# Edge loop of a four-layer GNN kernel: TensorE's transposes and second layer moved to the end of the loop body, blocks written out, one block bound loaded early

## The chip, the cores and the metric

One core of a Trainium2 chip runs one launch of the kernel. The metric is device time in microseconds (us) for the whole launch, the median of several runs. The engines are TensorE (PE; its weight loads are listed apart as PEld), VectorE (DVE), ScalarE (ACT), GpSimd (POOL) and SyncE (SP). Each engine has a sequencer that works through its instructions in order; the profile lists the sequencer's own work (register loads, branches) as PEldq, DVEq and ACTq. The engines tell each other of finished work by semaphores.

## What is computed

A residual network of four graph layers over 1024 nodes with 128 features and 16384 edges. The change lies in the stage that handles the edges, which serves all four layers:

```python
edge_index = jnp.stack([src, dst])
h = jnp.maximum(_layernorm(x), 0.0)
# layer 0, edge part: row = src, col = dst
m = jnp.concatenate([h[row], h[col]], axis=1)
m = relu(m @ Wm1 + bm1)
m = relu(m @ Wm2 + bm2)
m_sum = segment_sum(m, row, num_segments=1024)
# layer 1: attention over the edges, from edge counts per (src, dst)
# layer 2: mean over the first 10 edges of each source node
rank = arange(E) - starts[row_sorted];  keep = rank < 10
# layer 3: sum over the edges of edge_weight * x[src]
```

From the edges the kernel builds, beside `m_sum`, three dense tables over pairs of nodes: how many edges there are, how many of them are among a source's first ten, and the sum of their weights.

## The kernel before

**Staging.** The kernel first normalises `x` and sorts the edges by the block of 128 nodes in which their source lies (0 to 136 us of the span). A block's edges are padded to whole *pairs*: one pair is 2 x 128 edges. There are 8 blocks and, with this input, 68 pairs. Then the edge loop runs (150 to 573 us), and after it the node part of layer 0 and layers 1 to 3.

**The edge loop.** On TensorE, VectorE and ScalarE alike it is an outer loop over the 8 blocks with an inner loop over the block's pairs `g`, from `g0` to `end`. Both bounds are read from the tile `tabs` into registers by `value_load` at the start of each block. On TensorE and VectorE the outer loop is a loop of the machine (`eng.Fori(0, NB)`), and the place in `tabs` is itself worked out from the register `b`; on ScalarE the 8 blocks are written out by Python. GpSimd's part is written out over all pairs and has no blocks.

**TensorE, one pair** (lines 1195 to 1233): the transposes of pair `g+1`'s messages (L1140, into bank 6), the second layer of pair `g` (L1147 and L1148, into bank 7), `ranks` with `notbefb` (L1153, "ranks A", waits for `ranks_read`), a register load of the pair's `span` (L1204), `sources` for pair `g+2` (L1162, into bank 5), the inner loop that adds counts and weights into banks 0 to 3 (L1216 and L1219), the message sums (L1225, into bank 4), and `ranks` with `beforeb` for the next pair (L1153, "ranks B", signals `ranks_done`).

**VectorE, one pair**: reads the ranks (L880, waits for `ranks_restarted` and `ranks_done`, signals `ranks_read`), makes `OHc` (L885, L888), adds the bias to bank 7 (L891), makes the message of pair `g+2` (`message`, L864), and makes the next pair's one-hot tiles `OHs` (L900) and `OHd` (L905). **ScalarE, one pair**: `OHe` (L537), `OHs32` (L539), the two ReLUs (L549, L552).

**Between two blocks** the accumulated banks are emptied. ScalarE copies banks 2 and 3 (L557) and bank 4 (L558). VectorE copies banks 0 and 1 to `cntf` (L908, signals `counts_out`), makes `CT` (L911) and `SK` (L913), and waits for its own `kept_out`. TensorE waits for `counts_out` and `msum_out`, clears banks 0 to 4 with five matmuls by zeros (L1238), loads its two bounds (L1190, L1191) and restarts the ranks (L1153, signals `ranks_restarted`).

**The order** is that of the program text on each engine. No scheduler moves anything.

In the rows, tiles that share memory have the name of the larger one: `SK` is shown as `n1T`, the zeros as `hn`, bank tiles as `PS`, the gathered messages as `BT`.

Of the kernel before, what the change touches and what calls it, by code (L numbers as in the profile page):

```python
# [22 lines left out]
NB = N // P  # L23
# [3 lines left out]
NPAIR = E // PAIR + NB  # L27
# [30 lines left out]
def gnn_kernel(nc, I, out):  # L58
    ctx = ExitStack()
    with ctx:  # L60
        sems = {}

        def S(name):

            if name not in sems:
                sems[name] = ctx.enter_context(nc.semaphore(name))
            return sems[name]
# [180 lines left out]
        none = sb("none", [P, NB])  # L248
        lone = sb("lone", [P, P], bf16)
        zT = TT[0]  # L250

        block = ctx.enter_context(nc.Block())

# [204 lines left out]
        def _(eng):  # L458
# [74 lines left out]
            def scaled_onehots(g):  # L533
# [4 lines left out]
                eng.wait_ge(S("pair_done"), g + 1)  # L538
                a.activation(OHs32[:], OHs[:], ACT.Copy).then_inc(S("scaled_ready"), 1)  # L539

            for b in range(NB):
                g0 = eng.value_load(tabs[0:1, b:b + 1], min_val=0, max_val=NPAIR - 2)
                end = eng.value_load(tabs[0:1, b + NB:b + NB + 1], min_val=1, max_val=NPAIR - 1)
                with eng.Fori(g0, end) as g:
                    eng.wait_ge(S("src_onehots"), g + 1)
                    eng.wait_ge(S("counts_added"), g + 1)
                    scaled_onehots(g)
                    eng.wait_ge(S("m2_biased"), g + 1)
                    a.activation(m2s[:], m2s[:], ACT.Relu).then_inc(S("m2_ready"), 1)  # L549

                    eng.wait_ge(S("t_done"), g + 2)
                    a.activation(m1T[:].rearrange("p k e -> p (k e)"), bank(6), ACT.Relu).then_inc(S("m1_ready"), 1)  # L552

                eng.wait_ge(S("ranks_done"), end + 1)
                if b >= 2:
                    eng.wait_ge(S(f"spilled{b % 2}"), 16 * (b // 2))
                a.activation(TT[b % 2], bank(2, 2), ACT.Copy).then_inc(S("weights_out"), 1)  # L557
                a.activation(msum[:, :, b * P:(b + 1) * P], bank(4)[:, 0:F2].rearrange("p (f n) -> p f n", f=2),  # L558
                             ACT.Copy)\
                    .then_inc(S("msum_out"), 1)  # L560
            for b in range(NB):
                eng.wait_ge(S("SKT_done"), b + 1)
                a.activation(SKT[:, :, b * P:(b + 1) * P],
                             bank(6 + b % 2).bitcast(bf16).rearrange("p (j n) -> p j n", j=NB), ACT.Copy,
                             scale=1.0 / FRAC).then_inc(S("SKT_ready"), 1)
# [109 lines left out]
        def _(eng):  # L675
# [193 lines left out]
            eng.wait_ge(S("t_done"), 1)  # L869
            eng.wait_ge(S("pparts_done"), 2)  # L870
            v.tensor_tensor(MS[:], made, G[:, 1, :, :], ALU.add).then_inc(S("msg_ready"), 1)
            with eng.Fori(0, NB) as b:
                g0 = eng.value_load(tabs[0:1, bass.ds(b, 1)], min_val=0, max_val=NPAIR - 2)
                end = eng.value_load(tabs[0:1, bass.ds(b + NB, 1)], min_val=1, max_val=NPAIR - 1)
                with eng.Fori(g0, end) as g:

                    eng.wait_ge(S("ranks_restarted"), b + 1)
# [26 lines left out]
                    for k in range(2):  # L904
                        v.tensor_scalar(OHd[:, k, 0:N], iotaN[:], dstf[:, bass.ds(2 * g + 2 + k, 1)], None, ALU.is_equal)  # L905

                eng.wait_ge(S("ranks_done"), end + 1)
                v.tensor_copy(cntf[:], bank(0, 2)).then_inc(S("counts_out"), 1)  # L908
                eng.wait_ge(S("counts_out"), b + 1)
                ct = CT[:, bass.ds(b, 1), :].rearrange("p o n -> p (o n)")  # L910
                v.tensor_copy(ct, cntf[:]).then_inc(S("ct_out"), 1)  # L911
                eng.wait_ge(S("ct_out"), b + 1)
                v.tensor_tensor(SK[:, bass.ds(b, 1), :].rearrange("p o n -> p (o n)"), cntf[:], ct, ALU.subtract)\  # L913
                    .then_inc(S("kept_out"), 1)
                eng.wait_ge(S("kept_out"), b + 1)


            v.sem_inc(S("msg_ready"), NB)
            link(v.reciprocal(rden[:], Ur[:, :, D]))
# [126 lines left out]
        def _(eng):  # L1046
# [139 lines left out]
            transposes()  # L1186
            eng.wait_ge(S("turned_onehots"), 2)
            sources(1, second)
            with eng.Fori(0, NB) as b:
                g0 = eng.value_load(tabs[0:1, bass.ds(b, 1)], min_val=0, max_val=NPAIR - 2)  # L1190
                end = eng.value_load(tabs[0:1, bass.ds(b + NB, 1)], min_val=1, max_val=NPAIR - 1)  # L1191
                eng.wait_ge(S("src_onehots"), g0 + 1)
                ranks(((0, beforeb, 0), (1, onesb, 0), (1, beforeb, 1))).then_inc(S("ranks_restarted"), 1)
                with eng.Fori(g0, end) as g:
                    eng.wait_ge(S("m1_ready"), g + 1)
                    eng.wait_ge(S("msg_ready"), g + 2)
                    transposes()
                    second_layer(0)
                    second_layer(1).then_inc(S("m2_done"), 1)

                    eng.wait_ge(S("ranks_read"), g + 1)
                    ranks(((0, notbefb, 0), (0, onesb, 1), (1, notbefb, 1))).then_inc(S("ranks_added"), 1)
                    eng.wait_ge(S("spans"), 1)
# [28 lines left out]
                    eng.wait_ge(S("src_onehots"), g + 2)  # L1232
                    ranks(((0, beforeb, 0), (1, onesb, 0), (1, beforeb, 1))).then_inc(S("ranks_done"), 1)

                eng.wait_ge(S("counts_out"), b + 1)
                eng.wait_ge(S("msum_out"), b + 1)
                for k in range(5):
                    t.matmul(bank(k), zeros[:, 0:P], zeros[:, 0:BANK], start=True, stop=True)  # L1238

            eng.wait_ge(S("kept_out"), NB)  # L1240
            for b in range(NB):
# [244 lines left out]
```

## Time and profile before

| | |
|---|---|
| median of 3 runs | 1013.98 us (1013.17 to 1014.08) |
| profiled execution, its own time | 1013.37 us |
| its span, first to last instruction | 1011.5 us |
| PE busy | 834.6 us (83%) |
| DVE busy | 695.8 us (69%) |
| ACT busy | 476.0 us (47%) |
| mean granted TensorE clock | 0.947 of full |

The span is 1.9 us shorter than the execution's own time; what lies around it is not touched here. Busy times are means over stages with different limits, so the edge loop has to be read by itself, in order of time, on two or three engines at once. The words in brackets behind a row say how long the engine had been idle and what ended that; "issue" means that it waited for nothing that the profile knows as work, which in this kernel is mostly the engine's own sequencer with a register load or a branch.

### The profile page before, as it was taken

The numbers are of one execution on the slowest core, as the hardware profiler recorded it, in microseconds if no ns is written. First come the engines' busy times: TensorE is split into PE (matmuls) and PEld (weight loads), VectorE is DVE, ScalarE is ACT, GpSimd is POOL, SyncE is SP. The second block draws the span as 40 slices with busy tenths as digits, with TensorE's granted clock in tenths as the row PEclk, the third lists the DMA queues.
The fourth block names the chain that finished last, engine by engine and source line by source line (L and its number), as shares of the span: only waits on it lengthen the run. The fifth ranks groups of instructions, "written<-read, shape, count | busy, mean of one in ns | idle before, by whom it ended". The sixth has DMA issues, their size and how long they took to land.

```text
span 1011.5 us, 18259 instructions
## 1 busy us (share of the span) xinstructions
PE 834.6 (83%) x5207; PEld 523.3 (52%) x5236; DVE 695.8 (69%) x1803; ACT 476.0 (47%) x979; POOL 316.5 (31%) x424
## 2 busy tenths in 40 slices
PE   3999969989898989898989796877877766776658
PEld 2556738868787878686868644411142112311124
DVE  6399986666666666666666763699568875998451
ACT  5232105555555555564546655354544544445421
POOL 5030047545444545454535400122233120122000
PEclk9999969999999999999999999799879997999879
DMA  3120032111111111111112200000000000000300
GB/s 79 39 68 1 1 124 64 47 57 52 52 51 53 52 57 47 62 42 62 47 57 46 58 1 1 1 0 1 0 1 1 1 0 1 0 1 0 129 38 21
DMA packets 19139, 35.76 MB, mean 35 GB/s; under 512 B 5281, under 2 KB 11553, under 8 KB 18977
## 3 DMA queue, kind: packets, MB, share of 16 engines
q0 software_dynamic: 7104, 19.41, 6.7%
q1 hardware_dynamic: 12000, 15.95, 4.7%
q8 instruction: 15, 0.25, 0.1%
q14 instruction: 20, 0.16, 0.1%
HBM read 29.56 MB, written 5.79 MB: 35 GB/s over the span
## 4 chain that ended last, share of the span: by engine, by line
PE 63%; DVE 21%; ACT 6%; issue 5%; POOL 4%; DMA 0%; DVEq 0%; POOLq 0%; ACTq 0%
DVE OHd L964 9%; PE PS L1225 7%; PE PS L1147 6%; PE PS L1148 6%; PE PS L1219 5%; PE PS L1162 5%; DVE PS L975 5%; PE PS L1097 4%; PE PS L1337 4%; PE PS L1140 3%; PE PS L1262 3%; PE PS L1216 3%; PE PS L1153 2%; PE PS L1298 2%; PE PS L1328 2%
## 5 line engine op out<-in xcount | busy, mean ns | idle before, releaser
L390 POOL DMA_INDIRECT BT<-Qtab,gidx x148 | 150.5, 1017 | 96.3 <-DVE gidx L789 61.2
L537 ACT ACTIVATE OHe<-OHs,sew 128x128 bf16<-128x128 bf16 x408 | 126.7, 389 | 56.1 <-PE PS L1225 52.6
L404 POOL TENSOR_SCALAR KV<-BT,pid 128x256 bf16<-128x256 uint8 x74 | 70.3, 950 | 180.0 <-DVE MS L864 175.2
L964 DVE CUSTOM_DVE_ANT_0 OHd<-PS,n1T 128x1024 bf16<-128x1024 f32 x96 | 113.4, 1219 | 18.6 <-PE PS L1298 18.6
L549 ACT ACTIVATE m2s<-m2s 128x512 f32<-128x512 f32 x68 | 42.8, 630 | 119.1 <-DVE m2s L891 119.1
L1328 PE MATMUL PS<-rowA,sel 128*128 128x512 bf16 x177 | 57.9, 407 | 48.6 <-DVE PS L975 38.6
L443 POOL TENSOR_TENSOR zl<-AL,Sx 128x8 f32<-128x8 f32 x12 | 11.3, 946 | 258.7 <-DVE Sx L964 258.7
L891 DVE TENSOR_TENSOR m2s<-PS,bm 128x512 f32<-128x512 f32 x68 | 47.0, 691 | 59.0 <-PE PS L1148 58.8
L905 DVE TENSOR_SCALAR OHd<-iotaN,dstf 128x1024 bf16<-128x1024 f16 x136 | 64.6, 515 | 33.2 <-PE PS L1225 33.2
L1147 PE MATMUL PS<-Wm,m1T 128*128 128x256 f32 x272 | 83.8, 391 | 0.0
L1148 PE MATMUL PS<-Wm,m1T 128*128 128x256 f32 x272 | 82.6, 386 | 0.0
L1225 PE MATMUL PS<-OHs,m2s 128*128 128x128 f32 x544 | 78.1, 286 | 0.0
L630 ACT ACTIVATE Wn<-PS,s 128x1024 f32<-128x1024 f32 x48 | 53.1, 1113 | 49.3 <-PE PS L1328 49.1
L1097 PE MATMUL PS<-KV,m2s 128*128 128x288 f32 x256 | 72.8, 430 | 2.8 <-DVE KV L781 2.6
L1219 PE MATMUL PS<-OHd,OHe 128*128 x852 | 75.1, 220 | 0.0
L1328 PEld LDWEIGHTS PS<-rowA,sel 128*128 128x128 bf16 x192 | 11.8, 99 | 115.9 <-DVE PS L975 81.6
L864 DVE TENSOR_TENSOR MS<-PS,BT 128x512 f32<-128x512 f32 x68 | 47.0, 692 | 32.1 <-PE PS L1162 32.1
L1225 PEld LDWEIGHTS PS<-OHs,m2s 128*128 128x128 f32 x544 | 65.8, 191 | 5.1
L975 DVE SCALAR_TENSOR_TENSOR PS<-msum,s,BT 128x1024 f32<-128x1024 f32 x48 | 61.3, 1290 | 8.5 <-ACT cntf L630 5.2
L1162 PE MATMUL PS<-SKT,KV 128*128 (+1 forms) x420 | 59.4, 278 | 8.8 <-POOL KV L404 5.2
L1216 PE MATMUL PS<-OHd,OHc 128*128 x284 | 62.7, 221 | 4.4 <-issue 0.7
L781 DVE SCALAR_TENSOR_TENSOR KV<-iota,hi,carried 128x288 f32<-128x288 f32 x128 | 65.5, 512 | 0.0
(342 smaller groups left out, 1668.7 us busy)
## 6 DMA issues: line engine op xcount, KB each, us to landing
BT<-Wtab SPq DMA_DIRECT2D x1, 4096.0 KB, 12.9
BT<-Qtab,gidx POOLq DMA_INDIRECT x148, 2.8
BT<-Stab SPq DMA_DIRECT2D x1, 2048.0 KB, 10.2
Wtab<-H SPq DMA_DIRECT2D x4, 512.0 KB, 2.8
Wtab<-cs SPq DMA_DIRECT2D x4, 512.0 KB, 2.9
Qtab<-BT SPq DMA_DIRECT2D x1, 1024.0 KB, 4.5
Wn<-in_L_gnn_Wn SPq DMA_DIRECT2D x1, 1024.0 KB, 5.5
x<-in_x SPq DMA_DIRECT2D x1, 512.0 KB, 4.3
```

What stands on the lines that cost most here:

```text
L390: g.indirect_dma_start(out=G[:, p % SLOTS, k, :], out_offset=None, in_=Qtab, in_offset=bass.IndirectOffsetOnAxis(ap=gidx[:, p, k:k + 1], a ...
L537: a.activation(OHe[:, k, j, :], OHs[:, k, :], ACT.Copy, scale=sew[:, j, bass.ds(2 * g + k, 1)])
L964: v.tensor_tensor_reduce(junk[n % 2], bank(4, 2), mask[:, i, :], 1.0, 2 * FAR, ALU.subtract, ALU.max, Sx[:, i, hd:hd + 1]).then_inc(S("gat ...
L975: v.scalar_tensor_tensor(tile(hd, j), drow[hd], s8[:, j, hd:hd + 1], LNC[:, j, :], ALU.max, ALU.add).then_inc(S("gat_tt"), 1)
L1097: t.matmul(bank(5)[:, 0:2 * NCH], OHlo[:, i % RING, :], KV[:, i % RING, :, :].rearrange("p k c -> p (k c)"), start=(i == 0), stop=(i == T ...
L1147: t.matmul(to, m1T[:, k, :], Wm2[:, 0, :], start=True, stop=False)
L1148: return t.matmul(to, m1T[:, 2 + k, :], Wm2[:, 1, :], start=False, stop=True)
L1162: last = t.matmul(bank(5)[:, k * F2:(k + 1) * F2], OHsT[:, slot, k * P:(k + 1) * P], Pp[:, blk, j, :], start=(j == 0), stop=(j == 2))
L1216: t.matmul(PS[:, bass.ds(at, P)], OHc[:, k, :], dst, start=False, stop=False, skip_group_check=True)
L1219: t.matmul(PS[:, bass.ds(at + 2 * BANK, P)], OHe[:, k, j, :], dst, start=False, stop=False, skip_group_check=True)
L1225: last = t.matmul(bank(4)[:, f * P:(f + 1) * P], m2s[:, k, f * P:(f + 1) * P], OHs32[:, k, :], start=False, stop=False, skip_group_check=True)
L1328: last = t.matmul(tile(hd, j)[:, half * BANK:(half + 1) * BANK], sel[:, half, :], rowA[:, hd % 2, :], start=False, stop=False, skip_group_ ...
```

## The change

- On TensorE, the transposes and the second layer become a function `layers(g)`. It is called once ahead of the blocks with `g = 0`, and in the loop body for `g + 1` at the end, behind ranks B. The order of the work is the same around the loop; the place at which the loop closes, and at which a block ends, is now behind the second layer. Over the whole loop `layers` runs once more than before.
- On TensorE and VectorE the 8 blocks are written out by Python in place of the loop of the machine, as they were on ScalarE.
- All three engines load one bound per block in place of two: `g0` is the `end` of the block before. The load of the next block's `end` stands directly behind the inner loop, ahead of the waits that empty the banks. The place in `tabs` is a constant.

```diff
+        def last_pair(eng, b):
+            return eng.value_load(tabs[0:1, NB + b:NB + b + 1], min_val=1, max_val=NPAIR - 1)
...
 # VectorE (ScalarE likewise)
-            with eng.Fori(0, NB) as b:
-                g0 = eng.value_load(tabs[0:1, bass.ds(b, 1)], min_val=0, max_val=NPAIR - 2)
-                end = eng.value_load(tabs[0:1, bass.ds(b + NB, 1)], min_val=1, max_val=NPAIR - 1)
+            g0, end = 0, last_pair(eng, 0)
+            for b in range(NB):
                 with eng.Fori(g0, end) as g:
...
+                after = last_pair(eng, b + 1) if b + 1 < NB else None
                 eng.wait_ge(S("ranks_done"), end + 1)
                 v.tensor_copy(cntf[:], bank(0, 2)).then_inc(S("counts_out"), 1)
...
                 eng.wait_ge(S("kept_out"), b + 1)
+                g0, end = end, after
 # TensorE
+            def layers(g):
+                eng.wait_ge(S("m1_ready"), g + 1)
+                eng.wait_ge(S("msg_ready"), g + 2)
+                transposes()
+                second_layer(0)
+                second_layer(1).then_inc(S("m2_done"), 1)
+
+            layers(0)
+            g0, end = 0, last_pair(eng, 0)
+            for b in range(NB):
                 eng.wait_ge(S("src_onehots"), g0 + 1)
                 ranks(((0, beforeb, 0), (1, onesb, 0), (1, beforeb, 1))).then_inc(S("ranks_restarted"), 1)
                 with eng.Fori(g0, end) as g:
-                    eng.wait_ge(S("m1_ready"), g + 1)
-                    eng.wait_ge(S("msg_ready"), g + 2)
-                    transposes()
-                    second_layer(0)
-                    second_layer(1).then_inc(S("m2_done"), 1)
-
                     eng.wait_ge(S("ranks_read"), g + 1)
...
                     ranks(((0, beforeb, 0), (1, onesb, 0), (1, beforeb, 1))).then_inc(S("ranks_done"), 1)
+                    layers(g + 1)
+
+                after = last_pair(eng, b + 1) if b + 1 < NB else None
                 eng.wait_ge(S("counts_out"), b + 1)
                 eng.wait_ge(S("msum_out"), b + 1)
                 for k in range(5):
                     t.matmul(bank(k), zeros[:, 0:P], zeros[:, 0:BANK], start=True, stop=True)
+                g0, end = end, after
```

TensorE at the end of a block, before: from the message sums past the end of the inner loop (L1194) to the clearing matmuls (L1238) and the end of the outer loop (L1189).

```order
L1225 MATMUL PS<-OHs,m2s 128x128 x4
L1153 MATMUL PS<-OHs,beforeb 128x128
L1153 MATMUL PS<-OHs,onesb 128x128
L1153 MATMUL PS<-OHs,beforeb 128x128
L1194 REGISTER_ALU
L1194 COMPARE_AND_BRANCH
L1235 REGISTER_ALU
L1238 MATMUL PS<-hn 128x512 x5
L1189 REGISTER_ALU
L1189 COMPARE_AND_BRANCH
```

The same place after the change (the inner loop is now L1206, `value_load` L254, the clearing L1247):

```order
L1156 MATMUL PS<-OHs,beforeb 128x128
L1143 MATMUL PS<-ident,MS 128x128 x4
L1150 MATMUL PS<-Wm,m1T 128x256
L1151 MATMUL PS<-Wm,m1T 128x256
L1150 MATMUL PS<-Wm,m1T 128x256
L1151 MATMUL PS<-Wm,m1T 128x256
L1206 REGISTER_ALU
L1206 COMPARE_AND_BRANCH
L254 TENSOR_LOAD tabs
L254 ISA x2
L1247 MATMUL PS<-hn 128x512 x5
L1204 REGISTER_ALU
```

Transposes and second layer now stand between ranks B and the clearing; before, they stood behind the restart of the ranks in the next block.

VectorE at the end of a block, before:

```order
L875 COMPARE_AND_BRANCH
L907 REGISTER_ALU
L908 COPY cntf<-PS 128x1024
L909 REGISTER_ALU
L911 ISA
L911 COPY CT<-cntf 128x1024
L913 REGISTER_ALU
L913 TENSOR_TENSOR n1T<-cntf,CT 128x1024
L872 REGISTER_ALU
L872 COMPARE_AND_BRANCH
```

VectorE after the change (the inner loop is L879, the copies L913, L915 and L917):

```order
L879 COMPARE_AND_BRANCH
L254 TENSOR_LOAD tabs
L254 ISA x2
L912 REGISTER_ALU
L913 COPY cntf<-PS 128x1024
L915 CAST CT<-cntf 128x1024
L917 TENSOR_TENSOR n1T<-cntf,CT 128x1024
L879 UNCONDITIONAL_BRANCH
L882 REGISTER_ALU
```

The one load left stands ahead of the first copy; behind the last there is no load, and the jump back of the outer loop is gone.

## Rows read from the trace of the kernel before

**Rows 1.** Timeline of PE: start us, us, what, count, [idle before <- what ended it].

```profile
199.88 0.22 PE L1153 MATMUL PS<-OHs,beforeb 128*128 128x128 bf16 x1
...
202.22 0.22 PE L1153 MATMUL PS<-OHs,notbefb 128*128 128x128 bf16 x1
...
205.37 0.22 PE L1153 MATMUL PS<-OHs,beforeb 128*128 128x128 bf16 x1
...
207.39 1.02 PE L1238 MATMUL PS<-hn 128*128 128x512 bf16 x4 [1.70 <-DVE cntf L908]
...
209.50 0.23 PE L1153 MATMUL PS<-OHs,beforeb 128*128 128x128 bf16 x1 [1.08 <-issue]
...
212.02 0.22 PE L1153 MATMUL PS<-OHs,notbefb 128*128 128x128 bf16 x1
...
213.23 0.88 PE L1162 MATMUL PS<-SKT,KV 128*128 x6 [0.88 <-issue]
...
216.24 0.22 PE L1153 MATMUL PS<-OHs,beforeb 128*128 128x128 bf16 x1
```

**Rows 2.** Timeline of DVE: the same end of a block, and a pair in the third.

```profile
200.35 0.27 DVE L880 CUSTOM_DVE_ANT_0 prod<-OHs,PS 128x128 f32<-128x128 bf16 x1
...
205.84 1.21 DVE L908 COPY cntf<-PS 128x1024 f32<-128x1024 f32 x1
...
207.20 0.69 DVE L911 CAST CT<-cntf 128x1024 f32 x1
...
208.02 1.23 DVE L913 TENSOR_TENSOR n1T<-cntf,CT 128x1024 f32 x1
...
211.31 0.29 DVE L880 CUSTOM_DVE_ANT_0 prod<-OHs,PS 128x128 f32<-128x128 bf16 x1 [2.06 <-issue]
...
216.75 0.27 DVE L880 CUSTOM_DVE_ANT_0 prod<-OHs,PS 128x128 f32<-128x128 bf16 x1
...
260.48 0.29 DVE L880 CUSTOM_DVE_ANT_0 prod<-OHs,PS 128x128 f32<-128x128 bf16 x1 [2.04 <-issue]
...
266.26 0.27 DVE L880 CUSTOM_DVE_ANT_0 prod<-OHs,PS 128x128 f32<-128x128 bf16 x1
```

**Rows 3.** Waits, 150 to 572 us: engine line <- cause: us in total, times, longest.

```profile
DVE prod L880 <- issue: 15.8, 8, 2.1
```

**Rows 4.** DVE's sequencer, L872 to L875: count, ns min/median/max, first start, last start.

```profile
L875 DVEq COMPARE_BRANCH  x1: 50/50/50, 205.2 to 205.2; - x1
...
L872 DVEq FUSED_REGOPS  x1: 70/70/70, 209.6 to 209.6; - x1
...
L873 DVEq TENSOR_LOAD <-tabs x8: 301/306/566, 152.3 to 519.4; - x8
...
L874 DVEq FUSED_REGOPS  x2: 57/124/190, 210.3 to 210.7; - x2
...
L875 DVEq MOVE  x1: 43/43/43, 211.0 to 211.0; - x1
```

**Rows 5.** Timeline of PE and DVE at the first pair of the first block.

```profile
152.87 1.12 PE L1140 MATMUL PS<-ident,MS 128*128 128x128 f32 x4 [1.29 <-DVE MS L871]
...
154.32 0.29 DVE L880 CUSTOM_DVE_ANT_0 prod<-OHs,PS 128x128 f32<-128x128 bf16 x1 [1.51 <-issue]
...
156.94 0.22 PE L1153 MATMUL PS<-OHs,notbefb 128*128 128x128 bf16 x1
...
160.03 0.28 DVE L880 CUSTOM_DVE_ANT_0 prod<-OHs,PS 128x128 f32<-128x128 bf16 x1
```

**Rows 6.** Timeline of PE behind the last block.

```profile
573.70 1.07 PE L1245 MATMUL PS<-identb,n1T 128*128 128x128 bf16 x16 [0.90 <-DVE n1T L913]
```

**Rows 7.** Stretch: us, busy us (x) of PE, PEld, DVE, ACT, POOL, PEclk, DMA, GB/s.

```profile
258.50:262.50 4.00, 3.71 (x13) 3.10 (x14) 1.09 (x7) 0.00 (x0) 0.00 (x0) 0.57 0.11 32
```

**Rows 8.** DMA, 160 to 570 us: queue: packets, MB, share; issue: count, us to landing.

```profile
q14 instruction: 4, 0.03, 0.0%
...
BT<-Qtab,gidx POOLq DMA_INDIRECT x137, 2.8
```

More of the change, by code:

```diff
@@ L539, in scaled_onehots @@
                 a.activation(OHs32[:], OHs[:], ACT.Copy).then_inc(S("scaled_ready"), 1)
+            g0, end = 0, last_pair(eng, 0)
             for b in range(NB):
-                g0 = eng.value_load(tabs[0:1, b:b + 1], min_val=0, max_val=NPAIR - 2)
-                end = eng.value_load(tabs[0:1, b + NB:b + NB + 1], min_val=1, max_val=NPAIR - 1)
                 with eng.Fori(g0, end) as g:
@@ L909, in _ @@
                 eng.wait_ge(S("counts_out"), b + 1)
-                ct = CT[:, bass.ds(b, 1), :].rearrange("p o n -> p (o n)")
-                v.tensor_copy(ct, cntf[:]).then_inc(S("ct_out"), 1)
+                v.tensor_copy(CT[:, b, :], cntf[:]).then_inc(S("ct_out"), 1)
                 eng.wait_ge(S("ct_out"), b + 1)
-                v.tensor_tensor(SK[:, bass.ds(b, 1), :].rearrange("p o n -> p (o n)"), cntf[:], ct, ALU.subtract)\
-                    .then_inc(S("kept_out"), 1)
+                v.tensor_tensor(SK[:, b, :], cntf[:], CT[:, b, :], ALU.subtract).then_inc(S("kept_out"), 1)
                 eng.wait_ge(S("kept_out"), b + 1)
+                g0, end = end, after
             v.sem_inc(S("msg_ready"), NB)
@@ L1188, in _ @@
             sources(1, second)
-            with eng.Fori(0, NB) as b:
-                g0 = eng.value_load(tabs[0:1, bass.ds(b, 1)], min_val=0, max_val=NPAIR - 2)
-                end = eng.value_load(tabs[0:1, bass.ds(b + NB, 1)], min_val=1, max_val=NPAIR - 1)
+            def layers(g):
[5 more added lines that the diff above has]
+            layers(0)
+            g0, end = 0, last_pair(eng, 0)
+            for b in range(NB):
                 eng.wait_ge(S("src_onehots"), g0 + 1)
@@ L1233, in _ @@
                     ranks(((0, beforeb, 0), (1, onesb, 0), (1, beforeb, 1))).then_inc(S("ranks_done"), 1)
+                    layers(g + 1)
+                after = last_pair(eng, b + 1) if b + 1 < NB else None
                 eng.wait_ge(S("counts_out"), b + 1)
@@ L1238, in _ @@
                     t.matmul(bank(k), zeros[:, 0:P], zeros[:, 0:BANK], start=True, stop=True)
+                g0, end = end, after
             eng.wait_ge(S("kept_out"), NB)
```

## Prediction

> **What bounds the kernel now.** I read the edge loop in order of time, first TensorE, then VectorE over the same stretch, then VectorE's sequencer. Inside a block TensorE's matmuls follow each other with next to no gap: one pair takes 205.37 - 199.88 = 5.49 us from ranks B to ranks B [rows 1]. Across the end of a block the same distance is 216.24 - 205.37 = 10.87 us [rows 1], so emptying and restarting costs 5.4 us, seven times between 8 blocks. In that stretch TensorE waits three times: 1.70 us for `cntf`, 1.08 us and 0.88 us for its own sequencer [rows 1]. But TensorE is not what ends last there. VectorE copies from 205.84 to 209.25 without a gap that matters, and only at 211.31 reads the ranks of the next pair, after 2.06 us of "issue" [rows 2]. TensorE had restarted the ranks at 209.50 [rows 1], nearly 2 us earlier, and the transposes and second layer that it ran meanwhile held nobody up: ranks A at 212.02 came 0.71 us behind L880, and the span load and `sources` at 213.23 behind that [rows 1, 2]. So the chain over a block's end is: ranks B, VectorE's three copies, VectorE's two register loads, L880, ranks A. All eight such waits together are 15.8 us; the first is 1.51 us, so the seven between blocks are 2.04 us each [rows 3, 5].
>
> What the 2.06 us hold is seen in the sequencer. The copies end at 209.25; the jump of the outer loop is over at 209.6, the first load's part runs from there to 210.3, the second's to 211.0, and the set-up of the inner loop takes the last 0.3 us [rows 2, 4]. One load with its address and check is thus 0.7 us, of which 0.31 is the load itself.
>
> **Loads and jump on VectorE.** Behind the copies go both loads (2 x 0.7) and the outer jump. What stays is the wait for `kept_out` (about 0.1 of the 0.35 up to 209.6, my split) and the set-up of 0.3, so 0.4 in place of 2.06: 1.66 us less per block. One load comes back ahead of the first copy. The inner loop is left at 205.25 [rows 4]; 0.6 us (0.7 less the address, now a constant) make it 205.9, and a register operation and the start of the copy about 206.05, where the copy now starts at 205.84 [rows 2]. That is 0.2 us late. One of the eight loads took 0.57 in place of 0.31: the first, issued as VectorE had just begun a long operation [rows 4], and here L905 is running; with that the copy is 0.45 late. I take 0.3. The least is nothing, if the load lies wholly under L905. The most is a load that waits until L905 is through, which is at about 205.84: then the copy is 0.9 late. Net per block 1.66 - 0.3 = 1.35 us, from 0.75 to 1.66. Queued behind this load on VectorE are only the copies, and for them wait TensorE's clearing and, in the end, L880.
>
> **TensorE at the same place.** The question is whether it becomes the last. From ranks B to ranks A of a pair, with transposes and second layer between, it is 202.22 - 199.88 = 2.34 us [rows 1]. So the moved work ends at 205.37 + 2.34 = 207.71, later than the 207.39 at which clearing starts now, but it stands under VectorE's copies. The five clearing matmuls take 1.07 (four are 1.02 with the last one's tail), the ranks restart at 208.8, and L880 could start 0.47 later (199.88 to 200.35 [rows 1, 2]) at 209.25. VectorE gets there only at 211.31 - 1.35 = 209.95. TensorE has 0.7 us in hand. Its own load falls while the second layer runs. From L880 on everything depends on L880 as today: ranks A after 0.71, `sources` after 1.92, next L880 after 216.75 - 211.31 = 5.44 [rows 1, 2], because the layers, gone from this pair's front, were under that wait anyway. So their move gives nothing beyond letting VectorE's gain through: had they stayed, the second layer would end at 209.50 + 2.5 = 212.0 and hold ranks A there. **Both parts are needed, and together they give 7 x 1.35 = 9.5 us.** ScalarE's load lies in its wait for ranks B and costs nothing; GpSimd's order isn't touched.
>
> **Inside a block** the sequence is the same, with the jump now between second layer and ranks A. TensorE's sequencer runs ahead of the matmuls there, waiting for `ranks_read`. I count nothing.
>
> **The start.** Here the move costs. Before, the ranks of pair 0 were restarted ahead of the layers, while TensorE waited for the message (transposes at 152.87), and VectorE read them at 154.32 [rows 5]. Now the restart stands behind `layers(0)`, where ranks A stood, at 156.94; L880 comes 0.47 later at 157.4, and the next one 5.44 later at 162.85, against 160.03 [rows 5]: 2.8 us lost. From below: L880 is 3.1 us later, and ranks A of this pair comes at 158.1 in place of 156.94, 1.2 us; as the remainder had slack of its own I take 2.0 as the least, and 3.4 as the most.
>
> **The end.** `layers` runs once more behind the last ranks B, 2.3 us. By the times of block 0 the layers and the clearing are through 2.34 + 1.07 = 3.4 us behind ranks B. TensorE's next work waits for VectorE's last copy, `n1T` [rows 6], which is through 209.25 - 205.37 = 3.9 us behind ranks B [rows 1, 2] and has no load ahead of it in the last block. Cost nothing, with 0.5 us in hand.
>
> **The clock.** After two of the seven ends the granted clock fell for some 3.4 us; one stretch of 4 us shows 0.57 of full [rows 7], so 1.2 GHz for most of it, and the pair in it took 266.26 - 260.48 = 5.78 against 5.44, 0.34 us [rows 2]. The change leaves TensorE less idle at these places: the two falls may go (0.7 us less), or, as everything shifts, two others come (0.7 more). I count nothing.
>
> **Sum.** The profiled execution took 1013.37 us, 0.6 below the median of the runs: 1013.37 - 9.5 + 2.8 = 1006.7. Against the median it would be 0.6 more; I stay with the profiled one. Bounds: 1013.37 - 11.6 + 2.0 - 0.7 = 1003.1, and 1013.37 - 5.3 + 3.4 + 0.7 = 1012.2.
>
> **Rival 1: early loads are not early.** VectorE's load waits for L905, and TensorE's for its second layer (clearing at 208.4, L880 at 210.0 or later), so a good part of the 2.06 us is only moved: 0.75 per block, 1013.37 - 5.3 + 2.8 = 1010.9. For it: the one load of 0.57. Against: seven of eight, and that one too, took nothing like a whole operation. 0.12.
>
> **Rival 2, slower: code is fetched again.** Eight bodies stand where one stood on TensorE and VectorE. If a body lies across the border of two pieces of code and the jump back has to fetch the first again, every pair of that block pays. The nearest price of a small transfer is 2.8 us to landing [rows 8], the least nothing. One such block on one engine has 8.5 pairs: 24 us, 1030; from three paid fetches on, the 6.7 us are gone. Against: in 68 passes through three loops, ScalarE's written out eight times already, four packets of instructions came, 8 KB each [rows 8], so no loop fetched per pass. For: ScalarE's bodies are short. 0.06. The Trainium skill, Runtime: NRT & Kernel Launch, Instruction fetch mechanics, says that code comes in 16 KiB blocks, that two are held, and that a taken branch out of them stalls for a fetch. By that rule a body on TensorE that leaves the two would give this rival's time; the trace, with packets of 8 KB and none per pass, doesn't bear it out.
>
> **Rival 3: nothing to gain.** VectorE's copies are stretched, or the start costs over 5 us, so that within 0.2% nothing is left: 1012 to 1015. 0.04.
>
> **Chances.** Forecast 0.78 (1003.1 to 1010), rival 1 0.12, rival 2 0.06, rival 3 0.04. The range leaves out rivals 2 and 3 and the outer part of rival 1: 1003.0 to 1010.9. About 0.2%, 2 us, is what a measurement here can tell from no change. Faster: 0.78 + 0.09 = 0.87; same 0.06 (0.03 of each of rivals 1 and 3); slower 0.07.
>
> **What would show it.** L880 behind a block's end with an idle time of 0.4 us in place of 2.06, and 9.6 us behind the L880 before it in place of 10.96; `cntf` 0.2 to 0.45 us later behind ranks B; clearing right behind the second layer; the first L880 near 157.4 and the second near 162.9; ends of blocks that take 9.5 us on TensorE. It is wrong if L880 then waits for TensorE, if pairs inside a block take other than 5.4 to 5.5 us, or if instruction packets come by the dozen.

## The result

The change makes the kernel faster by 0.84%: 1005.11 us (median of 4 runs, 1004.71 to 1005.6) against 1013.59 us (4 runs, 1013.17 to 1014.08); the ratio is 0.9916, with a 95% interval from 0.9899 to 0.9934. The forecast was 1006.7 us in a range from 1003.0 to 1010.9. The profiled execution took 1005.0 us with a span of 1002.8 us, 8.7 us under that of before. The time came out near the forecast, in part by luck: the ends of blocks gave more than was forecast, a fallen clock took about as much, and 3 us came from outside the edited loop. Below these are taken apart.

The timeline of VectorE in the kernel after, at the end of block 0, answers to [rows 2]. Lines have moved: the read of the ranks is L884, the three copies are L913, L915 and L917.

```profile
202.74 0.28 DVE L884 CUSTOM_DVE_ANT_0 prod<-OHs,PS 128x128 f32<-128x128 bf16 x1
...
208.41 1.23 DVE L913 COPY cntf<-PS 128x1024 f32<-128x1024 f32 x1
209.67 0.69 DVE L915 CAST CT<-cntf 128x1024 int16<-128x1024 f32 x1
210.40 1.23 DVE L917 TENSOR_TENSOR n1T<-cntf,CT 128x1024 bf16<-128x1024 f32 x1
211.95 0.29 DVE L884 CUSTOM_DVE_ANT_0 prod<-OHs,PS 128x128 f32<-128x128 bf16 x1 [0.32 <-DVE n1T L917]
...
217.39 0.28 DVE L884 CUSTOM_DVE_ANT_0 prod<-OHs,PS 128x128 f32<-128x128 bf16 x1
```

The 2.06 us behind the copies are 0.32 us. From L884 to L884 across the end it is 211.95 - 202.74 = 9.21 us in place of 10.96. TensorE at the same place, which answers to [rows 1] (L1247 clears, L1156 are both kinds of ranks, L1165 the sources):

```profile
207.78 0.22 PE L1156 MATMUL PS<-OHs,beforeb 128*128 128x128 bf16 x1
...
207.95 0.61 PE L1143 MATMUL PS<-ident,MS 128*128 128x128 f32 x4
...
210.12 1.24 PE L1247 MATMUL PS<-hn 128*128 128x512 bf16 x5
...
211.20 0.22 PE L1156 MATMUL PS<-OHs,beforeb 128*128 128x128 bf16 x1
...
212.51 0.23 PE L1156 MATMUL PS<-OHs,notbefb 128*128 128x128 bf16 x1 [0.98 <-DVE rank L884]
...
213.88 0.88 PE L1165 MATMUL PS<-SKT,KV 128*128 x6 [1.04 <-issue]
```

Clearing follows the second layer without a gap, and the ranks are restarted (211.20) before VectorE is through with its copies (211.63). The waits of 1.70 us ahead of clearing and 1.08 us ahead of the restart are gone. In their place TensorE now idles 0.98 us between the restart and ranks A, where it had worked on the layers before, and then 1.04 us ahead of the sources (0.88 before). That turns out to matter.

At the start (answers to [rows 5]; the message tile that both kernels make there is at 152.14 in the one and 151.29 in the other):

```profile
151.29 0.67 DVE L876 TENSOR_TENSOR MS<-PS,BT 128x512 f32<-128x512 f32 x1
...
156.23 0.29 DVE L884 CUSTOM_DVE_ANT_0 prod<-OHs,PS 128x128 f32<-128x128 bf16 x1 [4.28 <-PE PS L1156]
...
162.70 0.29 DVE L884 CUSTOM_DVE_ANT_0 prod<-OHs,PS 128x128 f32<-128x128 bf16 x1
```

Where the 8.7 us of the span went, from the starts of L880 and L884, of the message tile and of the copy of the counts in the two timelines (the last pair up to that copy, 5.5 us in both, is left out):

| part | before | after | difference | forecast |
|---|---|---|---|---|
| up to the message tile of pair 1 | 152.1 | 151.3 | -0.8 | 0 |
| from there to the second read of the ranks | 7.9 | 11.4 | +3.5 | +2.8 |
| seven ends of blocks, read to read | 76.6 | 65.1 | -11.5 | -9.5 |
| the seven first pairs behind them | 38.8 | 41.2 | +2.4 | 0 |
| the other pairs | 289.4 | 289.3 | -0.1 | 0 |
| from the last copy of the counts to the end | 441.3 | 439.1 | -2.2 | 0 |

The first and the last part hold none of the edited code but the last copies, which are 0.2 us shorter, and under them the one run of `layers` that is new. The rest of these 3.0 us isn't explained, beyond that the stretches of low clock in layers 1 to 3 lie elsewhere. It isn't steady either: in the profile of the change that was taken again on another chip these two parts are 152.4 and 440.2 us, 0.8 us less than before in place of 3.0. So the loop gave 5.7 us, and 3 us came with it from outside.

### The profile page after: what moved, and what is told of

Read it like the earlier page. It is cut to its first block, busy times and chain, and to the rows that moved or that the text cites. A ratio compares the mean times of both kernels' runs of the same rounds, so it can differ in the third digit from the quotient of the medians.

```text
span 1002.8 us, 18140 instructions
## 1 busy us (share of the span) xinstructions
PE 841.4 (84%) x5247; PEld 525.7 (52%) x5248; DVE 696.8 (69%) x1802; ACT 475.6 (47%) x979; POOL 314.0 (31%) x424
## 3 DMA queue, kind: packets, MB, share of 16 engines
HBM read 29.56 MB, written 5.79 MB: 35 GB/s over the span
## 4 chain that ended last, share of the span: by engine, by line
PE 61%; DVE 23%; ACT 5%; POOL 4%; issue 4%; DMA 1%; DVEq 0%; POOLq 0%; ACTq 0%
DVE OHd L967 9%; PE PS L1231 7%; PE PS L1225 6%; PE PS L1150 5%; PE PS L1151 5%; PE PS L1165 5%; DVE PS L978 5%; PE PS L1100 4%; PE PS L1347 4%; PE PS L1222 3%; PE PS L1272 3%; PE PS L1143 3%; PE PS L1338 3%; PE PS L1308 2%; PE PS L1156 2%
## 5 line engine op out<-in xcount | busy, mean ns | idle before, releaser
L1338 PE MATMUL PS<-rowA,sel 128*128 128x512 bf16 x192 | 61.2, 405 | 45.6 <-DVE PS L978 37.4
L909 DVE TENSOR_SCALAR OHd<-iotaN,dstf 128x1024 bf16<-128x1024 f16 x136 | 64.1, 511 | 36.7 <-PE PS L1231 36.5
L1165 PE MATMUL PS<-SKT,KV 128*128 (+1 forms) x420 | 60.3, 280 | 14.6 <-issue 7.5
L1231 PEld LDWEIGHTS PS<-OHs,m2s 128*128 128x128 f32 x544 | 67.8, 196 | 6.4 <-issue 0.2
L1222 PE MATMUL PS<-OHd,OHc 128*128 x284 | 63.6, 224 | 3.4 <-issue 0.6
## 6 DMA issues: line engine op xcount, KB each, us to landing
BT<-Stab SPq DMA_DIRECT2D x1, 2048.0 KB, 10.3
```

Of the source, the lines that this page charges most:

```text
L1165: last = t.matmul(bank(5)[:, k * F2:(k + 1) * F2], OHsT[:, slot, k * P:(k + 1) * P], Pp[:, blk, j, :], start=(j == 0), stop=(j == 2))
L1222: t.matmul(PS[:, bass.ds(at, P)], OHc[:, k, :], dst, start=False, stop=False, skip_group_check=True)
L1231: last = t.matmul(bank(4)[:, f * P:(f + 1) * P], m2s[:, k, f * P:(f + 1) * P], OHs32[:, k, :], start=False, stop=False, skip_group_check=True)
L1338: last = t.matmul(tile(hd, j)[:, half * BANK:(half + 1) * BANK], sel[:, half, :], rowA[:, hd % 2, :], start=False, stop=False, skip_group_ ...
```

## The experiments

Kernels of one set ran on one chip beside the kernel before, and are compared by their ratio to it; the sets ran on different chips. The first set is the move alone, the bounds alone, the start put back and VectorE's load behind the copies; the second is the change again, the filled kernel, the blocks written out and the early span load with the bounds; the third is the early span load alone and the two combinations. Lengths from traces stand beside those of the one profile of the kernel before, from another chip. Lengths called "ends" and "first pairs" are, as in the table, from one read of the ranks to the next, across a block's end and behind it.

### The move alone

```diff
             sources(1, second)
+            layers(0)
             with eng.Fori(0, NB) as b:
                 g0 = eng.value_load(tabs[0:1, bass.ds(b, 1)], ...)
                 end = eng.value_load(tabs[0:1, bass.ds(b + NB, 1)], ...)
...
                 with eng.Fori(g0, end) as g:
-                    (transposes and second layer)
...
                     ranks(...).then_inc(S("ranks_done"), 1)
+                    layers(g + 1)
```

> Before, with the move of transposes and second layer alone; the outer loop and both register loads stay as they were. Theory 1 (VectorE's two loads end last at a block's end, the layers held nobody up): no gain at the seven block ends, L880 to L880 across them stays 10.9 us, and the start loses 2.4 to 2.8 us: 1016 us. Rival (TensorE was what ended last, and putting the layers under VectorE's copies is what saved the time): the block ends shrink by about 1.6 us each as in the change: 1005 to 1006 us.

Measured: 1026.13 us, ratio 1.0081 (1.0063 to 1.0098), slower than either theory. The timeline of VectorE at the first end:

```profile
210.93 1.21 DVE L908 COPY cntf<-PS 128x1024 f32<-128x1024 f32 x1
...
216.38 0.29 DVE L880 CUSTOM_DVE_ANT_0 prod<-OHs,PS 128x128 f32<-128x128 bf16 x1 [2.06 <-issue]
...
222.93 0.29 DVE L880 CUSTOM_DVE_ANT_0 prod<-OHs,PS 128x128 f32<-128x128 bf16 x1
```

TensorE at the same place; L908 begins at 210.93, so this is the stretch from the restart of the ranks to the sources:

```profile
214.87 0.23 PE L1153 MATMUL PS<-OHs,beforeb 128*128 128x128 bf16 x1 [0.80 <-issue]
...
216.94 0.23 PE L1153 MATMUL PS<-OHs,notbefb 128*128 128x128 bf16 x1 [1.74 <-DVE rank L880]
...
218.34 1.08 PE L1162 MATMUL PS<-SKT,KV 128*128 x6 [1.05 <-issue]
```

The stretch behind it, in the view by windows (columns as in [rows 7]):

```profile
218.80:222.20 3.40, 3.40 (x26) 3.00 (x26) 1.33 (x4) 0.75 (x3) 1.51 (x2) 0.51 0.00 0
```

The ends are as long as ever (76.5 us together), with the same 2.06 us: the move alone gives nothing there, so theory 1 held for the ends. And the pair behind takes 222.93 - 216.38 = 6.55 us in place of 5.44, with TensorE at 0.51 of its clock, the 1.2 GHz level. All seven first pairs are long, 6.4 to 7.3 us, 48.3 together where it was 38.8; the start cost 4.8 us more than before. TensorE had idled 0.80, 1.74 and 1.05 us just ahead of the fall.

### The bounds alone

```diff
-            layers(0)
             g0, end = 0, last_pair(eng, 0)
...
                 with eng.Fori(g0, end) as g:
+                    layers(g)
                     eng.wait_ge(S("ranks_read"), g + 1)
...
-                    layers(g + 1)
```

> The change without the move: blocks written out and one early load, but transposes and second layer at the front of the body as before. The prediction said that without the move the second layer would hold ranks A at the old time, so no gain: 1013 us. Theory 2, from the trace of the change: TensorE's own two loads (1.08 us idle before the restart) go too, so its second layer ends 1 us earlier and the sources, 1.93 us behind L880, are still what waits longest; then the block ends gain 1.6 to 1.7 us each without the move, and the start loses nothing: about 1002 us, less than the change.

Measured: 1003.61 us, ratio 0.9854 (0.9834 to 0.9875), nearly twice the gain of the change. Ends 64.5 us together, first pairs 38.7, and the second read of the ranks 7.6 us behind the message tile. TensorE's timeline at the first end:

```profile
209.38 1.03 PE L1245 MATMUL PS<-hn 128*128 128x512 bf16 x4 [1.81 <-DVE cntf L913]
...
212.58 0.22 PE L1156 MATMUL PS<-OHs,notbefb 128*128 128x128 bf16 x1
...
213.30 0.89 PE L1165 MATMUL PS<-SKT,KV 128*128 x6 [0.39 <-issue]
```

VectorE's timeline there, and under it the window from L884 on:

```profile
207.87 1.22 DVE L913 COPY cntf<-PS 128x1024 f32<-128x1024 f32 x1
...
211.41 0.29 DVE L884 CUSTOM_DVE_ANT_0 prod<-OHs,PS 128x128 f32<-128x128 bf16 x1 [0.32 <-DVE n1T L917]
```

```profile
211.40:217.00 5.60, 5.17 (x48) 4.19 (x47) 3.84 (x14) 2.09 (x6) 1.55 (x2) 1.00 0.02 7
```

With the layers at the front TensorE works through them while VectorE finishes its copies and reads the ranks; the sources start 213.30 - 211.41 = 1.89 us behind L884, as they did before (1.92), so the second layer does not hold them. It does hold ranks A, which come 212.58 - 211.41 = 1.17 us behind L884, where it is 0.56 in the change; but the sources go by TensorE's own sequencer and are no later for it. The gain of the change was the bounds, all of it. With the bounds in place the move costs time: the ratio of the change is 0.9916, and 0.9927 when it ran again, against 0.9854 here. No first pair shows a fallen clock in this kernel, where all seven do with the move alone on the same chip.

### The start put back

```diff
-            layers(0)
             g0, end = 0, last_pair(eng, 0)
             for b in range(NB):
                 eng.wait_ge(S("src_onehots"), g0 + 1)
                 ranks(...).then_inc(S("ranks_restarted"), 1)
+                if b == 0:
+                    layers(0)
```

> The change, with block 0's restart of the ranks (and its load) ahead of the first transposes and second layer, as before. If the late restart is what the start loses, L884 of the first pair comes back to about 2.2 us behind the message tile instead of 4.9, and the time falls by 2.4 to 2.8 us: 1002.5 us. If the loss has another source (a fallen clock, the written-out code), nothing changes: 1005 us.

Measured: 1010.58 us, ratio 0.9926 (0.9902 to 0.9951), no better than the change. But the step tested did hold: from the message tile to the second read of the ranks it is 8.1 us, where the change has 11.4.

```profile
152.85 0.67 DVE L876 TENSOR_TENSOR MS<-PS,BT 128x512 f32<-128x512 f32 x1
154.06 0.29 DVE L884 CUSTOM_DVE_ANT_0 prod<-OHs,PS 128x128 f32<-128x128 bf16 x1 [0.55 <-issue]
...
160.96 0.28 DVE L884 CUSTOM_DVE_ANT_0 prod<-OHs,PS 128x128 f32<-128x128 bf16 x1
```

Behind the ends it lost more than that against the profile of the change: ends 65.0 us, but first pairs 46.0 in place of 41.2, in six of seven with a fallen clock. Whether putting the start back brings these falls isn't shown: the change itself did not run on this chip, and the next kernel, which has the late start, has six falls there too. One of the six is 6.69 us long; the window over it:

```profile
212.30:219.00 6.70, 5.04 (x38) 4.36 (x39) 3.79 (x14) 2.56 (x7) 2.31 (x3) 0.76 0.01 2
```

### VectorE's load behind the copies

```diff
-                after = last_pair(eng, b + 1) if b + 1 < NB else None
                 eng.wait_ge(S("ranks_done"), end + 1)
...
                 eng.wait_ge(S("kept_out"), b + 1)
+                after = last_pair(eng, b + 1) if b + 1 < NB else None
```

> The change, with VectorE's one load behind its three copies instead of ahead of the first. If the load costs 0.6 to 0.7 us where it stands behind the copies and 0.15 us where it stands now (the copy starts 1.00 us behind L909 in place of 0.84), each of the seven ends is 0.45 to 0.55 us longer: 1008.5 us. If TensorE's restart were what L884 waits for, with VectorE early, nothing changes: 1005 us.

Measured: 1018.59 us, ratio 1.0 (0.9985 to 1.0015). The ends are 9.58 to 10.01 us, 67.8 together against 65.1: 0.39 us each, somewhat less than the 0.45 to 0.55 expected. The time is far from the one expected, which was a ratio of 0.995. VectorE's timeline at the first end:

```profile
213.61 1.23 DVE L916 TENSOR_TENSOR n1T<-cntf,CT 128x1024 bf16<-128x1024 f32 x1
215.79 0.29 DVE L884 CUSTOM_DVE_ANT_0 prod<-OHs,PS 128x128 f32<-128x128 bf16 x1 [0.95 <-PE PS L1156]
```

The idle time ahead of L884 is 0.95 us (0.32 in the change). The trace puts it down to TensorE's ranks, but their last matmul starts at 214.69 and takes 0.22, so it had been through for 0.88 us; it was the load. Of the other loss the first pairs, 44.2 us and six of seven with a fallen clock, hold 3.0 us against the change. The largest part, 5.2 us, lies behind the last copy of the counts (444.3 against 439.1 us) and isn't explained. So the early place of VectorE's load is worth 0.4 us per block, and TensorE's restart was not what L884 waited for.

### Filling TensorE's idle time

To test the clock as the cause, TensorE was given work that changes nothing: matmuls of zeros, added to banks 0 to 3. The change ran again beside it.

```diff
                 ranks(...).then_inc(S("ranks_restarted"), 1)
+                for i in range(10):
+                    t.matmul(bank(i % 4), zeros[:, 0:P], zeros[:, 0:BANK], start=False, stop=False,
+                             skip_group_check=True)
```

> The change itself, beside the runs below on one chip. 0.8% under the kernel before. Its pairs behind a block's end: 5.44 us where the clock stays at 2.4 GHz, 6.2 to 6.8 where it falls.

> The change, with ten matmuls that add zeros behind each restart of the ranks, 2.1 us of TensorE's time where it otherwise idles until the sources. Theory (moving the layers under the copies leaves TensorE idle behind the restart, the granted clock falls, and the pair that follows takes 1.1 to 1.8 us longer): no low stretch at block ends, first pairs back to 5.4 or 5.5 us each, so 2 to 7 us less than the change on the same chip, as many as it lost there. Rival (the long first pairs come from fetching the written-out code, or the clock falls for another reason): first pairs as in the change, no gain, or a loss of up to 0.3 us per block.

Measured: the change 1006.36 us, ratio 0.9927 (0.9909 to 0.9945); filled 1002.53 us, ratio 0.9898 (0.9881 to 0.9916). The medians differ by 3.8 us, while the two intervals just overlap. The 3.8 us are not the ends alone. Of the 5.2 us between the two spans the first pairs hold 1.4 and the stretch from the message tile to the second read of the ranks 1.2; 2.2 us lie outside the loop. In the profile the filled kernel has no stretch of low clock at any end, and first pairs of 5.45 to 5.79 us, 38.8 together (the change beside it: 40.2, one fall). The window of the filled kernel behind the first end, where TensorE's busy time has the zeros in it:

```profile
211.00:216.30 5.30, 5.20 (x47) 3.65 (x46) 3.38 (x13) 1.86 (x5) 1.35 (x2) 1.00 0.01 5
```

One profile of each isn't much: the change had two falls in its first profile and one in this. Against the rival of fetched code it is clear: the filled kernel has the same bodies, with the zeros added, and no first pair over 5.8 us.

### The blocks written out alone

```diff
-            with eng.Fori(0, NB) as b:
-                g0 = eng.value_load(tabs[0:1, bass.ds(b, 1)], ...)
-                end = eng.value_load(tabs[0:1, bass.ds(b + NB, 1)], ...)
+            for b in range(NB):
+                g0 = eng.value_load(tabs[0:1, b:b + 1], ...)
+                end = eng.value_load(tabs[0:1, b + NB:b + NB + 1], ...)
```

The places of `CT` and `SK` are constants there too, as in the change.

> Before, with the blocks written out on TensorE and VectorE and nothing else: two loads per block at its start, from constant places, layers at the front. The outer jump (0.35 us), the address operations (0.1 each) and those of the copies (0.2) go: the ends take 10.3 us in place of 10.94, 4 us in all, 1013.4 us where the kernel before has 1017.5. If fetching the written-out code costs as much as that, no change.

Measured: 1006.35 us, ratio 0.9936 (0.9916 to 0.9956), 5.9 us less. The ends are 10.2 to 10.3 us, 71.5 together: 5.1 us less. VectorE's timeline at the first end:

```profile
205.04 1.21 DVE L908 COPY cntf<-PS 128x1024 f32<-128x1024 f32 x1
...
207.01 1.23 DVE L912 TENSOR_TENSOR n1T<-cntf,CT 128x1024 bf16<-128x1024 f32 x1
209.81 0.29 DVE L880 CUSTOM_DVE_ANT_0 prod<-OHs,PS 128x128 f32<-128x128 bf16 x1 [1.58 <-issue]
```

Behind the copies 1.58 us are left of 2.06, and the copies take 3.20 us in place of 3.41. Writing the blocks out therefore gives a good 0.7 us of the 1.7 per end, and carrying one bound and loading it early the other 0.9 to 1.0.

### The span load

In the time from the read ranks to the count matmuls TensorE's sequencer loads the pair's `span`. That load does not depend on the ranks.

```diff
-                    eng.wait_ge(S("ranks_read"), g + 1)
-                    ranks(((0, notbefb, 0), (0, onesb, 1), (1, notbefb, 1))).then_inc(S("ranks_added"), 1)
                     eng.wait_ge(S("spans"), 1)
                     span = eng.value_load(rngi[0:1, bass.ds(g, 1)], ...)
+                    eng.wait_ge(S("ranks_read"), g + 1)
+                    ranks(((0, notbefb, 0), (0, onesb, 1), (1, notbefb, 1))).then_inc(S("ranks_added"), 1)
```

It was first tried on the kernel with the bounds alone, then on the kernel before.

> The kernel with the bounds alone (layers in front), and in it the load of the pair's span moved ahead of the wait for the ranks. Sources then no longer start 1.93 us behind L884 in the first pair of a block but when the second layer is through, 0.3 us sooner; inside a block the count matmuls lose the 0.08 us that TensorE waits for its sequencer: 2 us from the first pairs and up to 5 from the 60 others, 997 to 1001 us where the kernel with the bounds alone has 1003.6. If the sequencer has no slack to give, no change.

> Before, with nothing but the load of the pair's span moved ahead of the wait for the ranks. Theory (inside a block TensorE's sequencer, not its matmuls, set the pair: from the read ranks through the load and the register operations to the count matmuls): the 60 pairs fall from 5.47 to 5.15 us and the first pairs by 0.65, 23 to 25 us in all: 988 us where the kernel before has 1012. Rival (the 40 us of the earlier run came from the load's place together with the early bounds): under 10 us.

Measured: with the bounds 972.62 us, ratio 0.9605 (0.9585 to 0.9624), far beyond what was expected; alone 990.88 us, ratio 0.9777 (0.9758 to 0.9796), 22.5 us less and so just short of the 23 to 25 expected. Inside a block the kernel with the bounds and the early span (VectorE's timeline):

```profile
215.06 0.27 DVE L884 CUSTOM_DVE_ANT_0 prod<-OHs,PS 128x128 f32<-128x128 bf16 x1
...
220.21 0.27 DVE L884 CUSTOM_DVE_ANT_0 prod<-OHs,PS 128x128 f32<-128x128 bf16 x1
...
225.36 0.27 DVE L884 CUSTOM_DVE_ANT_0 prod<-OHs,PS 128x128 f32<-128x128 bf16 x1
```

One pair is 5.15 us (220.21 - 215.06) in place of 5.47. The first transposes of the table behind the loop start at 533.5 us where they start at 564.6 with the bounds alone. Of these 31.1 us the 52 pairs inside blocks hold 22.0, the first pairs 5.1 and the ends 2.8. Some 3 us of the 22.0 don't belong to the span load: the three pairs with twice as many count matmuls took 7.9 us in every kernel of the first set and 6.9 in the change on both other chips, for a reason that isn't known. By the ratios (0.9854 to 0.9605) the span load is worth 2.5%, 25 us. The groups of L1216 in the kernel before and of L1222 in this one, over the whole loop, show what had been waited for (count | busy, mean ns | idle ahead, and its cause):

```profile
L1216 PEld LDWEIGHTS PS<-OHd,OHc 128*128 128x128 f16 x276 | 26.7, 97 | 22.2 <-issue 22.1
```

```profile
L1222 PEld LDWEIGHTS PS<-OHd,OHc 128*128 128x128 f16 x276 | 27.0, 98 | 2.5 <-issue 1.9
```

22 us in which the weight load waited for the sequencer are 2. That is 0.3 us per pair, as much as the pair became shorter. So in the kernel before, the count matmuls followed the chain "L880, ranks read, span load, register operations", and not the matmuls ahead of them. With the span load alone the clock fell at four of the seven ends, though the layers stand at the front there; three of the first pairs take 7.1 us where three others take 4.8. The window at the end of block 1 in that kernel:

```profile
250.80:257.60 6.80, 5.85 (x23) 4.63 (x24) 2.06 (x9) 0.45 (x2) 0.00 (x0) 0.50 0.16 54
```

It still has TensorE's two loads and its waits at the ends. So the fall isn't tied to the place of the layers alone. Nor is it tied to how long TensorE idles at an end in all. The kernel before idles 3.6 to 3.7 us at most ends and fell at two of seven, the move alone idles 3.6 and fell at all seven; the bounds alone idle 2.2 and never fell, the start put back idles 2.0 to 2.5 and fell at six, and the last two ran on one chip. What decides it stays open.

### Two combinations

The first is the change with block 0's restart put back, the span load early, and eight matmuls of zeros behind each later restart. The second has in addition, at a block's end:

```diff
 # TensorE
-                for k in range(5): (clear bank k), then ranks restart
+                (clear bank 4), ranks restart, then for k in range(4): (clear bank k)
 # VectorE
-                CT and SK behind the copy of the counts
+                CT and SK behind OHs in the next block's first pair, written out ahead of the loop
```

> The change with block 0's restart ahead of its layers, the span load ahead of the wait for the ranks, and eight matmuls that add zeros behind each later restart. With the clock kept up and the span loaded early, nothing is left against the layers at the end: TensorE is clear of them when the ranks are read, so sources start about 1.3 us behind L884 in place of when the second layer is through: 0.2 to 0.5 us per block under the kernel with bounds and span, 3 us in all: 0.958 of before. If the clock falls, 0.965.

> As the run before, and at a block's end TensorE clears bank 4 alone, restarts the ranks and clears banks 0 to 3 behind that (two matmuls of zeros instead of eight), while VectorE makes CT and SK of a block inside the next block's first pair, written out ahead of the loop. L880's counterpart can then start 2.4 us behind the copy of the counts in place of 3.5; the 2 us of copies come back in the first pair, where VectorE has 1.2 us of slack. Expected 0.5 to 1.2 us per block less than the run before: 0.950 to 0.955 of before. If VectorE's late start in the second pair gives it all back, as the run before.

Measured: 965.24 us, ratio 0.9533 (0.9509 to 0.9557), and 964.72 us, ratio 0.9516 (0.9499 to 0.9533). Neither profile has a low clock at an end. In the first, ends are 60.5 us together and first pairs 33.5; it gained more than was expected, 0.7% over the early span load with the bounds where 0.3% was expected. Most of that lies inside blocks: 265.1 us in place of 270.5, a pair of 5.00 us in place of 5.15. With the layers in front the transposes start 214.70 - 214.44 = 0.26 us behind ranks B, and with the layers at the end 208.86 - 208.69 = 0.17, so with the span load early the move does gain inside a block. That the loop's jump, which stood between ranks B and the transposes, is the reason was not tested apart. In the second the ends fall to 51.7, but the first pairs rise to 44.5. VectorE's timeline of the second behind the first end:

```profile
201.38 1.23 DVE L927 COPY cntf<-PS 128x1024 f32<-128x1024 f32 x1
203.77 0.29 DVE L888 CUSTOM_DVE_ANT_0 prod<-OHs,PS 128x128 f32<-128x128 bf16 x1 [1.16 <-PE PS L1168]
...
207.11 0.89 DVE L879 CAST CT<-cntf 128x1024 int16<-128x1024 f32 x1
208.03 1.23 DVE L881 TENSOR_TENSOR n1T<-cntf,CT 128x1024 bf16<-128x1024 f32 x1
...
209.97 0.28 DVE L888 CUSTOM_DVE_ANT_0 prod<-OHs,PS 128x128 f32<-128x128 bf16 x1
```

VectorE reads the ranks 203.77 - 201.38 = 2.39 us behind the start of the copy of the counts, where the first combination needs 3.53 (200.95 to 204.48), 1.1 us less, and then pays the two copies in the pair: the gain is given back, to within the intervals. The two are 4.7 and 4.8% under the kernel before, and some 4% under the change by the ratios.

## Why the prediction was right, and where it was wrong

**The ends of blocks.** VectorE's sequencer was what ended last, and taking its loads away was the gain; the late load shows the price of a place, the bounds alone show the whole. TensorE was through in time, as forecast: it restarted the ranks 0.75 us ahead of L884. The term was sized 1.35 us per block and measured 1.64. The copy of the counts starts 5.67 us behind the last read of the ranks (208.41 - 202.74) where it was 5.49, so 0.18 late and not 0.3; the three copies are 0.19 us shorter, which the sum left out (with the blocks written out alone, and the same constant places, they are 0.21 shorter); and what stays behind them is 0.32 and not 0.4. Against that three of the seven ends are 0.3 to 0.4 us longer than the others. At the end of block 1 the wait ahead of L884 is 0.72 us (VectorE's timeline):

```profile
259.81 0.29 DVE L884 CUSTOM_DVE_ANT_0 prod<-OHs,PS 128x128 f32<-128x128 bf16 x1 [0.72 <-DVE n1T L917]
```

**"Both parts are needed" was wrong**, and it is the step that failed. It held the second layer's end at the old time had the layers stayed, and forgot that TensorE's own two loads, 1.08 us ahead of its restart [rows 1], would be gone too. The bounds alone measured the full gain at the ends, 64.5 us against 65.1. The 0.71 us by which ranks A followed L880 had a little of the layers in it as well: with the layers gone from there it is 0.56.

**The start.** 2.8 us were forecast, 3.5 measured; the way was right, as the kernel with the start put back shows. The first read of the ranks came 4.9 us behind the message tile, where 5.3 was forecast, but the pair behind it took 6.47 us in place of 5.44. What was missing is the clock: behind the late restart TensorE idled, and the clock that had risen fell again, as the same window of the kernel before and of the change shows:

```profile
158.00:162.00 4.00, 3.83 (x37) 3.49 (x35) 2.87 (x12) 3.15 (x9) 3.46 (x5) 1.00 0.26 85
```

```profile
158.00:162.00 4.00, 3.83 (x28) 3.42 (x28) 1.48 (x5) 1.21 (x3) 3.33 (x5) 0.57 0.27 91
```

In the filled kernel, whose clock stays up in this window, that pair takes 5.89 us.

**The clock at the ends** was counted at nothing, with 0.7 us to either side, and the text expected less idle time on TensorE. The idle time did fall, but it moved: from ahead of the clearing, with the layers behind, to the stretch behind the restart, with little work around it. In the profiled execution two of seven first pairs ran at the low level, no more than before, but with the fall at a dearer place; one of them took 469.70 - 463.20 = 6.50 us (VectorE's timeline, then the window over it):

```profile
463.20 0.29 DVE L884 CUSTOM_DVE_ANT_0 prod<-OHs,PS 128x128 f32<-128x128 bf16 x1 [0.32 <-DVE n1T L917]
...
469.70 0.29 DVE L884 CUSTOM_DVE_ANT_0 prod<-OHs,PS 128x128 f32<-128x128 bf16 x1
```

```profile
465.00:470.00 5.00, 4.85 (x38) 4.46 (x39) 2.35 (x8) 2.39 (x7) 2.15 (x3) 0.66 0.00 0
```

In kernels with the move a fall costs 0.7 to 1.9 us (first pairs of 6.2 to 7.3 us against 5.44), not the 0.34 that [rows 2, 7] had shown. Before, the stretch at half clock lay over the layers and began ahead of L880 [rows 2, 7]; now it begins behind the restart's waits and lies over the counts and message sums. The first pairs cost 2.4 us in this profile, 1.4 in the one taken again, and 9.5 with the move alone. This term was mis-sized, in the direction of a loss.

**Inside a block** the forecast of no change was right (289.3 against 289.4 us). The reading behind it, that TensorE's matmuls bound the pair, was not: its sequencer did, and the 22.2 us of "issue" at the weight loads of the count matmuls in the kernel before would have shown it.

**The end of the loop** cost nothing, as forecast, but with 0.15 us in hand and not 0.5: clearing is through at 566.77, VectorE's last copy at 566.92. **The rivals:** no load waited for its engine to run dry (rival 1): VectorE's load began at 207.7 while L909 was running, and so did TensorE's beside its message sums and ranks B (the sequencers' rows of the change, 200 to 212 us):

```profile
L254 PEldq TENSOR_LOAD <-tabs x1: 303/303/303, 207.7 to 207.7; - x1
L254 DVEq TENSOR_LOAD <-tabs x1: 314/314/314, 207.7 to 207.7; - x1
```

Code was fetched in the loop, ten packets against the four of [rows 8], but not per pass (DMA queues of the change, 160 to 562 us: packets, MB, share):

```profile
q8 instruction: 4, 0.07, 0.1%
q14 instruction: 6, 0.05, 0.0%
```

Whether the three longer ends, and a first pair of 5.88 us at full clock behind the end of block 4, are such fetches stays open; their sum is under 2 us.

**The sum** was right in its result because 2 us more at the ends and 3 us from outside the loop more than made up for 0.7 us at the start and 2.4 us of clock. That is luck: the loop alone gave 5.7 us where 6.7 were forecast.

## What to carry to other kernels

Follow a loop through the engines' sequencers too: a register load or a jump behind a wait is on the path of everything after it, and one that does not depend on the wait belongs ahead of it (here 0.3 us per pair, 2.2% of the kernel, by moving two lines up). When work is moved off a stretch, ask what the engine does there now: on TensorE the idle time left behind can cost more by the clock than the move gives (the move alone gave nothing at the ends and lost 9.5 us in the pairs behind them). Test the parts of a change apart, for a sum that comes out right doesn't show that its terms are.

## What the runs showed of the hardware

- TensorE's clock fell to the 1.2 GHz level at ends at which it had been idle several times in a row (0.80, 1.74 and 1.05 us ahead of the fall at 218.8 in the move alone), though not at every such end. A fall cost 0.3 us of a pair of 5.4 in the kernel before, 0.7 to 1.9 in kernels with the move, and up to 2.3 of one of 4.8 with the early span load. Matmuls of zeros in the idle time went along with its staying up at all seven ends (one profile each of three kernels with such matmuls).
- A load of one bound from a constant place into a register occupies a sequencer for 0.6 us, of which the load itself is 0.31 (L254 in the change, 207.7 to 208.3); the outer loop's jump and the address operations, those of the copies among them, cost 0.7 us per block (the blocks written out alone).
- A sequencer's register load runs beside its engine's work: on VectorE at 207.7 while L909 ran, on TensorE at 207.7 while the message sums and ranks B ran.
